# Gram products spread over a head's four groups, and ScalarE's tap products, casts of x and copies of built taps at other places in its order

## What is computed

```python
x = x + attention(_gn(x))      # k, v: 1x1 projection, then 3x3 depthwise; q: wavelet transform,
                               # 3x3 depthwise on its bands, inverse transform
x = x + conv_net(_gn(x))       # sign, 3x3 conv with binary weights, batch norm, twice, plus identity

# inside attention, per head of 16 channels, over the 9216 pixels:
q = q / max(norm(q), eps); k = k / max(norm(k), eps)
attn = softmax(einsum('bhdn,bhen->bhde', q, k) * temperature)
out = einsum('oc,bchw->bohw', proj_w, einsum('bhde,bhen->bhdn', attn, v))
```

## Time and profile before

| | us |
|---|---|
| median of 3 runs | 1437.34 |
| lowest, highest | 1431.96, 1441.17 |
| the profiled execution | 1437.24 |
| its span | 1435.7 |

### The profile page before, as it was taken

One profiled execution on the slowest core, in us unless ns is written; L12 is line 12 of the kernel. 1 busy time (PEld: TensorE's weight loads), 2 busy tenths in 40 slices (PEclk: granted clock), 3 DMA queues, 4 the chain that ended last, 5 costly groups with the idle time before them and its releaser, 6 DMA issues. The chain is left out here.

```text
span 1435.7 us, 36598 instructions
## 1 busy us (share of the span) xinstructions
PE 1176.2 (82%) x12644; PEld 927.6 (65%) x12644; DVE 1013.7 (71%) x1771; ACT 881.4 (61%) x1574; POOL 423.6 (30%) x473
## 2 busy tenths in 40 slices
PE   0999908899999899999999999636999997999900
PEld 0555507789899898998989899512555554555500
DVE  6677407899999899998999889246767654063394
ACT  0677826778888788886888787110442453766383
POOL 6100023446545455545546445102000010000000
PEclk9999957999999999999999999858999999999955
DMA  9966792344445344444445342157777330000079
GB/s 332 416 283 269 302 176 71 88 124 119 111 128 140 95 124 128 105 128 121 110 128 136 93 128 72 34 227 270 272 249 261 112 137 1 0 1 0 1 276 398
DMA packets 148704, 221.26 MB, mean 154 GB/s; under 512 B 115624, under 2 KB 116788, under 8 KB 144192
## 3 DMA queue, kind: packets, MB, share of 16 engines
q1 hardware_dynamic: 137456, 152.26, 35.0%
q0 software_dynamic: 6480, 47.19, 8.7%
q10 hardware_dynamic: 4608, 19.67, 3.9%
HBM read 131.84 MB, written 87.20 MB: 153 GB/s over the span
## 5 line engine op out<-in xcount | busy, mean ns | idle before, releaser
L1670 PE MATMUL b_conv_bank<-b_sign,wsign 128*128 (+1 forms) x1728 | 296.2, 328 | 10.5 <-ACT b_sign L1450 7.9
L757 POOL TENSOR_TENSOR b_vacc<-b_vacc 128x576 f32<-128x576 f32 x128 | 180.2, 1408 | 332.3 <-ACT b_vacc L850 331.5
L1670 PEld LDWEIGHTS b_conv_bank<-b_sign,wsign 128*128 128x128 bf16 x1728 | 168.4, 98 | 141.2 <-issue 28.5
L989 PE MATMUL b_bank<-b_yh,b_tmh 96*96 96x200 f16 x768 | 197.3, 257 | 39.0 <-DVE b_feat L954 20.1
L989 PE MATMUL b_bank<-b_tkh,b_kt 96*96 96x100 f16 x1536 | 226.8, 212 | 2.3 <-DVE b_tml L970 2.3
L991 PE MATMUL b_bank<-b_tkh,b_kt 96*96 96x100 f16 x1536 | 226.1, 212 | 0.0
L990 PE MATMUL b_bank<-b_tkl,b_kt 96*96 96x100 f16 x1536 | 226.1, 212 | 0.0
L947 DVE SCALAR_TENSOR_TENSOR b_value_sum<-b_vin,b_vtaps,b_value_sum 128x576 f32<-128x576 f32 x256 | 207.1, 809 | 0.0
L989 PEld LDWEIGHTS b_bank<-b_tkh,b_kt 96*96 96x96 f16 x1536 | 196.7, 128 | 3.9 <-DVE b_tml L970 2.5
L1469 ACT CAST b_y<-b_conv_bank 128x384 f32 (+1 forms) x192 | 91.3, 477 | 174.5 <-PE b_conv_bank L1670 172.3
L991 PEld LDWEIGHTS b_bank<-b_tkh,b_kt 96*96 96x96 f16 x1536 | 196.9, 128 | 0.0
(11 more groups left out here) (212 smaller groups left out, 2517.0 us busy)
## 6 DMA issues: line engine op xcount, KB each, us to landing
b_vin<-value_projection_scratch SPq DMA_DIRECT2D x32, 686.0 KB, 5.5
keys_scratch<-b_khl SPq DMA_DIRECT2D x24, 784.0 KB, 3.4
value_projection_scratch<-b_vout ACTq DMA_DIRECT2D x24, 784.0 KB, 4.6
b_kt<-keys_scratch SPq DMA_DIRECT2D x128, 147.0 KB, 2.9
b_xraw<-in_x SPq DMA_DIRECT2D x128, 144.0 KB, 5.0
values_scratch<-b_vacc SPq DMA_DIRECT2D x32, 576.0 KB, 3.2
b_values<-values_scratch SPq DMA_DIRECT2D x48, 384.0 KB, 3.9
out<-xs SPq DMA_DIRECT2D x25, 576.0 KB, 7.1
```

Of the source, the lines that this page charges most:

```text
L757: nc.gpsimd.tensor_tensor(whole, whole, room, ALU.add).then_inc(s_padd, 1)
L989: nc.tensor.matmul(out, w_hi, m_hi, start=first, stop=False)
L1670: ins = nc.tensor.matmul(cbank[k % NBK][:, 0:CH].rearrange("p (r c) -> p r c", c=W), p["wsign"][nth // NIMG][:, t * C:(t + 1) * C], padded ...
```

## The change

- `NO_TAP`: VectorE's tap that stood behind job 9 stands behind job 8.
- `HIGH_X`: the two casts of x on ScalarE go from jobs 13 and 14 to 10 and 12. `PRODUCTS`: the two later tap products of the next group's first half go from jobs 12 and 15 to 13 and 16. In GpSimd's body `low_x` stands ahead of `add_product` in each of the two rounds.
- `PIECES` in place of `START` and `PER`: sum 0 has 7, 7, 7, 7, 11, 11 matmuls in pieces 0 to 5, sum 1 has 3, 3, 7, 7, 7, 7, 16 in pieces 6 to 12. `COPY_AT` goes from 5, 11, 14 to 5, 12, 14, `NULL_AT` from 12 to 13.
- ScalarE copies the eight built taps ahead of its first three tap products at the block's start, and SyncE issues each slab right behind the rows and keys of its group.

```diff
--- before.py
+++ after.py
@@ -540,10 +540,10 @@
             "kg s1 mq u tk",
             "kg s1 mq u mq",
         )
-        NO_TAP = (2, 4, 6, 8, 12, 14, 16, 18)
+        NO_TAP = (2, 4, 6, 9, 12, 14, 16, 18)
         TAPS = 6
-        NORMALISE, HIGH_X = (4, 6, 7, 8), (13, 14)
-        FIRST_TAP, PRODUCTS = (1, 11), (2, 5, 12, 15)
+        NORMALISE, HIGH_X = (4, 6, 7, 8), (10, 12)
+        FIRST_TAP, PRODUCTS = (1, 11), (2, 5, 13, 16)
         LAG = {"s1": 0, "kg": 0, "u": 1}
         tk_jobs, mq_jobs = iter(range(NTK)), iter(range(NTM))
         jobs = []
@@ -625,7 +625,6 @@
             for i in range(2):
                 load_rows(xraw, d["x_rows"], s_xin, i, i)
                 load_keys(i, i)
-            for i in range(2):
                 load_slab(i * SLAB * WP, i)
 
             def body(k, i, image, ahead):
@@ -768,8 +767,8 @@
                         edges(head, (k // GPH - 1) % 2, i, k % GPH, n)
                 if how != LAST:
                     for n in range(2):
+                        low_x(i + 1, (k + 1) % 2, n)
                         add_product(i + 1, (k + 1) % 2, 0, n)
-                        low_x(i + 1, (k + 1) % 2, n)
 
             pool.wait_ge(s_c, 7 * 16)
             spread_taps(0, 0)
@@ -816,8 +815,9 @@
                     b[0:W, 0:nb * n * wide].rearrange("p (b m o) -> p b m o", b=nb, m=n))
 
         units = [[(2 * e + im, blk) for im in range(2) for blk in range(S2B // RUN)] for e in range(GPARTS - 1)]
-        PER = 10
-        START, COPY_AT, NULL_AT = [0, 6], [5, 11, 14], 12
+        PIECES = [{0: 7, 1: 7, 2: 7, 3: 7, 4: 11, 5: 11}, {6: 3, 7: 3, 8: 7, 9: 7, 10: 7, 11: 7, 12: 16}]
+        COPY_AT, NULL_AT = [5, 12, 14], 13
+        assert all(sum(counts.values()) == len(unit) for counts, unit in zip(PIECES, units))
 
         def chunk(k, n):
 
@@ -902,12 +902,12 @@
                 normalise(0, 0, 1, im)
             for part in range(2):
                 high_x(0, 0, part)
+            for m, (kind, j) in enumerate(lead):
+                act.wait_ge(s_pe, m + 1)
+                nc.scalar.copy(*built(kind, j, 0, 0, bank[m % NB])).then_inc(s_hi, 1)
             first_tap(0, 0, 1)
             for t in (1, 2):
                 tap_product(0, 0, 0, t, False)
-            for m, (kind, j) in enumerate(lead):
-                act.wait_ge(s_pe, m + 1)
-                nc.scalar.copy(*built(kind, j, 0, 0, bank[m % NB])).then_inc(s_hi, 1)
             body(0, 0, 0, FIRST)
             level(act, s_hi)
             for i in range(1, PEEL):
@@ -1089,9 +1089,10 @@
                         piece, parity = chunk(k, n), (k // GPH - 1) % 2
                         if piece == 0:
                             need(at["u", GC - 1])
-                        for e, first in enumerate(START):
-                            if first <= piece and (piece - first) * PER < len(units[e]):
-                                gram_part(gram, parity, e, (piece - first) * PER, (piece - first + 1) * PER)
+                        for e, counts in enumerate(PIECES):
+                            if piece in counts:
+                                done = sum(many for other, many in counts.items() if other < piece)
+                                gram_part(gram, parity, e, done, done + counts[piece])
                         if piece == NULL_AT:
                             gram_null(gram)
```

## The result

The changed kernel takes 1472.77 us (median of 4 runs, 1471.52 to 1474.81) where the kernel before takes 1437.11 (4 runs): a ratio of 1.0253, interval 1.0221 to 1.0285. It is slower by 35.7 us, where 20 were forecast (1457), and lies 0.8 us above the stated range. The profiled execution took 1473.83 us, its span is 1472.3.

A forecast was written before the change was run, and what follows sets the result against it. Groups of 21.0 us were held set not by TensorE (82% busy) but by another chain, VectorE waiting for ScalarE's casts. 1437.24 + 24.5 (copies, net) + 10.5 (clock) - 9 (start) - 5.6 (first groups) = 1457.6, said 1457; range 1441 to 1472.

The forecast's parts named there:

- the stalls at the copies: ScalarE waits at two Gram-sum copies per head, in second and fourth groups; net of savings +3.5 a head, +24.5 us.
- start and first groups: Earlier first tap at the block's start, -9 us, and four groups ahead of the first Gram products, -5.6 us.
- 1.15 us saved in each of 28 groups: Moved products and casts of x remove VectorE's gaps at jobs 12, 13, 15; bounds 0.9 and 1.3 us a group.
- its cover is 1.3 us: GpSimd's changed order is hidden: second product ready at T+14.7, before low 16 at T+16.0.
- about 4 x 19.9: Length of a head's four groups with Gram products spread, without anything else, in us.
- 7 x 8.1 = 56.7 for the stalls: Seven heads, each losing 4.0 us in the second group and 4.1 us in the fourth, before savings.
- the first stall: Second group: ScalarE's copy waits behind job 10's cast, VectorE gets job 11 3.5 us later; costs 4.0 us.
- The clock term: TensorE's waits around the stalls lower its clock: 14 x 0.75 = +10.5 us, bounds 0 and 14 x 2.4.
- The clock holds: Rival: the stalls come but TensorE's clock stays up; 1447 us, chance 0.25.
- Faster, the copy finds the sum complete: Rival: nothing stands behind the copy, all 28 groups run at 19.9 us; 1390 us, chance 0.08.
- Long clock losses: Rival: lowered TensorE clock costs 2.4 us at each stall; 1481 us, chance 0.12.
- The moves do nothing: Rival: moved products and casts save nothing, gaps turn up elsewhere, stalls come; 1489 us, chance 0.05.

## Why the prediction went wrong

The direction and the stalls at the copies were right. The size was not, +35.7 us for +20, because the saving that was set against the stalls was put at 32 us where 10 came.

**Right: the copies.** The prediction had ScalarE stand 3.2 us at each of 14 copies, for the sums' last matmuls four jobs ahead of it. The waits are 3.19 and 3.17, and the low parts behind them start at T+14.6 and T+9.8 (T is the group's start) where 14.75 and 9.85 were worked out. Without them the time is 1412 (copies later), so the whole loss hangs on two numbers of `COPY_AT`.

**Right in the sum, in part by luck: start and first groups.** They were to save 9 and 5.6, 14.6 together. The first low part of a job (the second line here, VectorE's timeline) comes at 212.22 for 222.07:

```profile
211.29 1.01 DVE L947 SCALAR_TENSOR_TENSOR b_value_sum<-b_vin,b_vtaps,b_vacc 128x576 f32<-128x576 f32 x1 [4.05 <-POOL b_vacc L756]
212.22 0.56 DVE L954 TENSOR_TENSOR b_feat<-b_bank,b_feat 96x400 f16<-96x400 f32 x1
```

And the fifth group begins at 298.15 for 312.78: 14.6. The start's share is 9.85 of it, and 4.8 are left for the four groups. There the 4 x 1.15 did not come: the third and fourth last 20.42 and 20.43, 0.57 under 21.0 and not 1.15. That is 2.3 for four groups; 1.5 came from the clock of the third and fourth (0.97 and 0.96, now 1.00) where 1 was forecast, and the last 1.0 from the first two, by what isn't shown. So the errors cancelled. That the start alone keeps only 5 to 6 us was not foreseen.

**Wrong: 1.15 us saved in each of 28 groups, 28 x 1.15 = 32.** Behind the first four groups the kernel with the copies later keeps 1437.1 - 14.6 - 1412.3 = 10 us of the 32 (11 by the windows). This is the term that failed, by 22 us, in two places. ScalarE's part of it came as worked out: VectorE's gaps at jobs 12, 13 and 15 are gone, and with GpSimd's old order an undisturbed group lasts 19.7. But the prediction let GpSimd's changed order pass with "its cover is 1.3 us". That cover holds for what waits for GpSimd's results. It says nothing of an instruction on VectorE that runs at the same time, and the tap behind job 10 grew by 0.72: 20.42 where 19.85 was said. Giving GpSimd its old order back is worth 12 of the 22 us (1412.3 to 1400.2). The other 10 lie in the second and fourth groups, for which "about 4 x 19.9" a head took the same saving as for the others. They last 20.66 and 20.95 even with GpSimd's old order, only 0.5 and 0.1 less than before, where, by the rows, a copy and a tap product stand together ahead of a cast. The changed kernel's own copies stand one place sooner, and there this part can't be told from the stalls.

**Wrong in its split: the stalls.** Forecast 7 x 8.1 = 56.7 for the stalls and 10.5 for the clock, 67.2 together; measured 60.4, which takes 7 off the error of 22 and leaves the 15 by which the forecast was short. Of these 46 are the stalls (23.68 - 20.44 and 24.52 - 20.44 in the run with TensorE kept busy make 7.3 a head, 51 in all; the groups with copies later are themselves 0.2 and 0.5 above 20.44, 5 in all) and 14.5 for the clock. Part of the first stall covers what GpSimd costs the tap there: VectorE's gap is 2.64, not 3.5. The clock term was sized at 0.75 us per stall. In the profiled executions a fourth group that no turn falls on loses 1.8 on average (25.3 to 26.9, for 24.52), a second one 0.9 (between 0 and 1.8).

The sum then stands: 1437.1 - 14.6 - 10 + 46 + 14.5 = 1473. It closes by construction, since the last three terms are differences of measured medians; what checks it is that the windows, up to the last group's start, give 11, 43 and 17 for them.

**The rivals.** "The clock holds" is out for 11 stalls of 14 (the run with TensorE kept busy is what it would have looked like, and it is 14.5 us faster). "Faster, the copy finds the sum complete" was wrong for this kernel, but moving the copies gives just that case: 1412, and 1400 with GpSimd's old order, 10 above its 1390. "Long clock losses" (2.4 us each) was nearer for the fourth groups than the 0.75 taken, and far off over all 14 (34 us for 14.5). "The moves do nothing" is out: with the copies later the groups behind the first four keep 10 us, and VectorE's gaps are gone.

**Not tried.** No run of the start alone kept the clock up in the first groups, so how much of the start's gain the clock took isn't shown.

## What to carry to other kernels

When work is moved on one engine and its reader's place is numbered by the same function on another, compare the two orders instruction by instruction: "chunk 5" was behind job 10 for the reader and behind job 14 for the writer, and one place decided between 1.7% faster and 2.5% slower. An in-order engine that waits early holds all that stands behind it, and short waits of the matmul engine in a row then can cost clock on top (14.5 us here). And "hidden, since nobody waits for it" is not the end of the question for a moved instruction on GpSimd: ask also which VectorE instruction with two SBUF inputs runs at its new time.

## What was not expected of the hardware

- A VectorE instruction with both inputs in SBUF took 1.53 us in place of 0.81 beside a GpSimd instruction that reads SBUF, and 0.81 beside GpSimd's memsets. A low part, with one input in PSUM, kept its 0.56 beside the reading one.
- Three TensorE waits of 0.98, 0.54 and 0.78 us were followed by the lower clock. Three of 1.06, 0.67 and 0.49 us were so in one second group and not in another. Matmuls without use in those waits kept the clock at 1.00 and made the kernel 14.5 us faster.
